# Sixteen heads of 8: rounds of two steps, the two second products behind each other, and one job of 128 rows per round

## The chip, the cores and the metric

The program runs on one core of one Trainium2 chip. The time is the device time of one execution in microseconds (us), the median of three runs. Five engines of the core take part, each with its own queue of instructions: TensorE (PE; PEld are its weight loads), ScalarE (ACT), VectorE (DVE), GpSimd (POOL) and SyncE (SP), which starts most DMAs.

## The reference

A stack of eight layers over `x` (16 batches, 256 tokens, 128 features), alternately attention with a context `ctx_512` (16 batches, 1601 keys, 64 features) and a feed-forward layer. The change touches three of the attention layers, those with 16 heads of 8:

```python
# first: causal self-attention and cross attention, added before the output projection
q, k, v = heads(x @ Wq + bq), heads(x @ Wk + bk), heads(x @ Wv + bv)
att = where(causal, einsum('bhqd,bhkd->bhqk', q, k) * scale, -inf)
y = einsum('bhqk,bhkd->bhqd', softmax(att), v)
qc, kc, vc = heads(x @ Wcq + bcq), heads(ctx @ Wck + bck), heads(ctx @ Wcv + bcv)
y = y + einsum('bhqk,bhkd->bhqd', softmax(einsum('bhqd,bhkd->bhqk', qc, kc) * scale), vc)
return y @ Wp + bp
# second and fourth: the cross part alone
```

Each is applied to the normalised `x` and added to it. The other layers (two experts' stages, a quantised convolution, an attention with heads of 32 and its own feed-forward parts, a shared expert) are not touched.

## The kernel before, in words

`attention8` writes one such layer; it is called three times, as stages a0 (with causal attention), a1 and a3 (cross attention alone). A quad is 4 heads; there are 4 quads for each source of keys. A step is one tile of 128 keys of one quad, against all 256 queries: 13 tiles for the context (the last has 65 keys) and 2 for the layer's own tokens. So a batch has 52 steps, or 60 in a0.

What a step does, with its letter in the plan:

- "scores" (L598 to 612): four matmuls of 64 contracted rows and 256 columns, on two halves of the array (`a` = 0, 1), transposed scores of 4 heads, into two of three score banks. They wait until ScalarE has done all halves up to the first one of the step before: `pe.wait_ge(S["probs"], 2 * e.i - 1)` (L602). With the split in three bf16 parts and a row for minus the maximum in the contraction, they come out shifted.
- The exponentials (L681 to 690): ScalarE takes each half, 128 x 512, from its bank into one of four buffers of probabilities.
- "pv" (L613 to 628), the second product, fp32: four matmuls, each on its own 32 columns of the array and all 128 rows, 9 outputs (8 and the sum) by 256 queries, added up in one bank over a quad. In the order before it comes `LAG8` = 3 steps after its scores. At a quad's end ScalarE copies the bank (L695).

Beside the steps runs the search for the maxima, a quad or so ahead. A "unit" (L575 to 597) is a matmul of 63 rows and 512 key columns into one of three banks, and VectorE reduces it to a column of maxima (L747). There are 26 per cross quad (24 full ones and two narrow ones, L738), two per step. After a quad's last unit VectorE forms minus the maxima (L751), TensorE transposes them (the job "turn", L635), ScalarE copies them (L701) and starts a DMA into the operand of the scores (L679).

All other matmuls are "jobs" that share one bank, `side_bank`: keys and values of the next batch from its context ("k_cross" L640, "v_cross" L644, with 64 rows, on one half of the array), and jobs of 128 rows: "turn", "x_turned" L649, "q" L652, "k_own" L654, "v_own" L657, "quad_out" (L662, transposes a quad's outputs), "heads_turned" L665, "proj" L668. Each waits until the one before it has been evacuated (L631, the semaphore `side_done`), by ScalarE (L696 to 726), or for "quad_out" and "proj" by VectorE (L769 to 792).

The order is a list of events that `schedule8` builds once; each engine walks the same list and takes what is its own. `segment8` writes one batch's part: for every step n its scores, two units, the second product of step n - 3, further units, then what was put at n. Jobs are placed by numbers of steps, so two or three can stand between two second products and the next scores, and keys and values come every second step. GpSimd splits keys and queries in bf16 parts (L512 to 518), SP writes and restacks them in DRAM.

## Time and profile before

| | us |
|---|---|
| runs | 7690.1, 7738.05, 7750.57 |
| median | 7738.05 |
| span of the profiled execution | 7680.6 |
| TensorE / VectorE / ScalarE / GpSimd busy | 6854.6 / 5897.9 / 4972.7 / 2316.8 |
| mean granted clock of TensorE | 0.951 |

The profile is of one execution of its own; of that one only the span, from its first to its last instruction, is given, and no time beside it. The runs are other executions. Busy times are sums over the span in which the union of an engine's instructions is counted; a matmul's end is modelled. Reductions of VectorE and exponentials of ScalarE overlap by some 0.05 to 0.1 us in the records, so starts are better than durations for a cadence.

### The profile page before, as it was taken

What the parts mean: (1) busy time and instruction counts of PE and PEld (TensorE: products, weight loads), DVE (VectorE), ACT (ScalarE), POOL (GpSimd) and SP (SyncE); (2) the same over time, 40 slices, a digit from 0 to 9 for tenths busy, and PEclk for the clock granted to TensorE, in tenths of its full rate; (3) what the DMA queues carried; (4) which work ended last, traced back from release to release, by engine and by line L of the source; (5) the groups of instructions that cost most, each with busy time, mean ns of one, the idle gap of its engine ahead of it and who ended that gap; (6) DMA issues with size and microseconds to landing.
All of it is one profiled execution on the core that took longest, in us unless ns stands there. A gap on an engine that the chain in (4) does not pass through costs nothing. (4 is left out here: it accounts for less than half of the span.)

```text
span 7680.6 us, 186325 instructions
## 1 busy us (share of the span) xinstructions
PE 6854.6 (89%) x73814; PEld 3108.2 (40%) x73814; DVE 5897.9 (77%) x12885; ACT 4972.7 (65%) x9846; POOL 2316.8 (30%) x2368
## 2 busy tenths in 40 slices
PE   6999999977999998788769999999996889999979
PEld 2333333343333333344424444444444433333335
DVE  6888888846898997788757777777774488999955
ACT  4787788834888886455446666666653168888842
POOL 1222222111211210155435555555554112212100
PEclk9999999987999999899879999999998589999989
DMA  5344444104434341100100000000001144343400
GB/s 101 86 98 94 94 91 94 44 27 84 95 78 103 81 92 44 28 18 17 40 22 10 9 8 10 6 10 9 5 5 56 28 103 99 75 103 85 85 26 12
DMA packets 319830, 417.82 MB, mean 54 GB/s; under 512 B 56533, under 2 KB 238054, under 8 KB 318969
## 3 DMA queue, kind: packets, MB, share of 16 engines
q1 hardware_dynamic: 317432, 405.36, 23.2%
q8 instruction: 595, 9.75, 0.6%
q14 instruction: 267, 2.18, 0.1%
q10 hardware_dynamic: 1536, 0.53, 0.0%
HBM read 225.41 MB, written 174.66 MB: 52 GB/s over the span
## 5 line engine op out<-in xcount | busy, mean ns | idle before, releaser
L688 ACT ACTIVATE a_probs<-scores_ps 128x512 f32<-128x512 f32 (+2 forms) x5248 | 2821.1, 591 | 356.9 <-PE scores_ps L608 263.7
L747 DVE TENSOR_REDUCE a_unit_max<-bank 128x1 f32<-128x512 f32 x3072 | 2003.7, 683 | 180.2 <-PE bank L595 145.3
L625 PE MATMUL bank<-a_probs,a_v_sb 128*9 128x256 f32 (+1 forms) x20992 | 1615.8, 380 | 29.3 <-ACT a_out_sb L695 20.3
L1299 ACT ACTIVATE cross_probs<-scores_ps 128x512 f32<-128x512 f32 (+1 forms) x1792 | 868.6, 571 | 590.4 <-PE scores_ps L1194 590.4
L608 PE MATMUL scores_ps<-a_stack 64*128 64x256 bf16 (+1 forms) x10496 | 1131.7, 275 | 60.9 <-ACT a_probs L688 55.9
L1381 DVE TENSOR_REDUCE cross_unit_max<-bank 128x1 f32<-128x512 f32 x1536 | 979.2, 685 | 253.3 <-PE bank L1180 250.2
L747 DVE TENSOR_REDUCE a_unit_max<-scores_ps 128x1 f32<-128x512 f32 x1536 | 1049.8, 683 | 160.4 <-PE scores_ps L595 143.1
L595 PE MATMUL bank<-a_stack 63*128 63x512 bf16 (+2 forms) x3413 | 1039.7, 372 | 7.4 <-DMA a_stack<-a_stack_dram 2.1
L1465 POOL TENSOR_TENSOR cross_added<-cross_probs 128x1024 f32<-128x1024 f32 x384 | 905.6, 2358 | 327.3 <-PE bank L1227 241.5
L608 PEld LDWEIGHTS scores_ps<-a_stack 64*128 64x128 bf16 (+1 forms) x10496 | 373.3, 96 | 991.1 <-ACT a_probs L688 831.7
L512 POOL CAST a_parts<-a_qk 128x512 bf16<-128x512 f32 (+3 forms) x225 | 117.7, 523 | 1893.8 <-ACT a_qk L707 1814.2
L595 PE MATMUL scores_ps<-a_stack 63*128 63x512 bf16 (+2 forms) x1707 | 635.7, 372 | 49.2 <-DMA a_stack<-a_stack_dram 45.9
L625 PEld LDWEIGHTS bank<-a_probs,a_v_sb 128*9 128x9 f32 (+1 forms) x20992 | 317.1, 88 | 700.2 <-ACT a_probs L688 397.1
L1191 PE MATMUL scores_ps<-cross_qk_f 32*128 32x256 f32 x6656 | 559.2, 394 | 8.6 <-ACT cross_probs L1299 8.5
L1218 PE MATMUL bank<-cross_probs,cross_v_sb 128*32 128x256 f32 x6656 | 452.3, 386 | 0.0
L1180 PE MATMUL bank<-cross_qk_b 32*128 32x512 bf16 x1536 | 390.4, 382 | 59.0 <-DVE cross_unit_max L1381 53.9
L805 POOL TENSOR_SCALAR_AFFINE_SELECT a_probs<-a_probs 128x512 f32<-128x512 f32 x128 | 81.3, 635 | 1014.1 <-ACT a_probs L688 1012.9
L595 PEld LDWEIGHTS bank<-a_stack 63*128 63x128 bf16 x3413 | 289.8, 94 | 185.6 <-DVE a_unit_max L747 59.5
L1191 PEld LDWEIGHTS scores_ps<-cross_qk_f 32*128 32x128 f32 x6656 | 312.5, 181 | 62.2 <-issue 28.7
L1194 PE MATMUL scores_ps<-cross_negmax_row,cross_ones_b 1*128 1x256 bf16 (+1 forms) x3328 | 297.2, 270 | 0.0
L1485 POOL CAST cross_qk_b<-cross_qk_f 128x1024 bf16<-128x1024 f32 (+1 forms) x128 | 109.1, 852 | 451.3 <-ACT cross_qk_f L1326 257.3
L640 PE MATMUL bank<-a_ctxT,a_wk_c_by_dim 64*128 64x512 f32 (+1 forms) x384 | 197.1, 595 | 52.6 <-DVE a_attn L779 24.4
(421 smaller groups left out, 10031.3 us busy)
## 6 DMA issues: line engine op xcount, KB each, us to landing
a_stack_dram<-a_parts SPq DMA_DIRECT2D x288, 400.2 KB, 4.3
a_stack<-a_stack_dram SPq DMA_DIRECT2D x256, 348.2 KB, 8.0
a_stack<-a_stack_dram SPq DMA_DIRECT2D x128, 444.2 KB, 9.9
a_ctxT<-in_ctxT SPq DMA_DIRECT2D x48, 400.2 KB, 4.8
a_stack_dram<-a_parts SPq DMA_DIRECT2D x288, 64.0 KB, 2.4
a_stack_dram<-a_parts SPq DMA_DIRECT2D x96, 128.0 KB, 2.4
f_x<-x_after_dram SPq DMA_DIRECT2D x32, 256.0 KB, 3.3
x_after_dram<-a_res SPq DMA_DIRECT2D x48, 128.0 KB, 4.3
```

The costliest lines, as they stand in the source:

```text
L595: ins = pe.matmul(bank[:, 0:n], stack[b][rows(a, 63), 2 * e.g + j, c0 + qt * P:c0 + (qt + 1) * P], stack[b][rows(a, 63), 2 * e.g + j, k0:k ...
L608: ins = pe.matmul(score_bank[(2 * e.i + a) % 3][0:n, j * TOK + q0:(j + 1) * TOK], stack[p][rows(a, 64), 2 * e.g + j, k0:k0 + n], stack[p][ ...
L625: ins = pe.matmul(out_bank[32 * h:32 * h + V8, q0:TOK], v[0:n, e.t, 4 * e.g + h, :], A.probs[0:n, held, o + q0:o + TOK], start=(e.t == 0), ...
L688: act.activation(by_pair(A.probs[0:n, b, a * 512:(a + 1) * 512])[:, :, q0:TOK], by_pair(score_bank[(2 * e.i + a) % 3][0:n, :])[:, :, q0:TO ...
L747: ins = dve.tensor_reduce(unit_max[:, e.g % 2, qt, 2 * a + j, c:c + 1], bank[:, 0:e.s.chunks[c][1]], AX.X, ALU.max)
L1180: ins = pe.matmul(bank[:, 0:n], q[rows(h), qt * P:(qt + 1) * P], k[rows(h), c0:c0 + n], start=True, stop=True)
L1191: pe.matmul(score_bank[h][0:n, m * TOK:(m + 1) * TOK], k[rows(h), k0:k0 + n], q[rows(h), :], start=True, stop=False, skip_group_check=True)
L1194: ins = pe.matmul(score_bank[h][0:n, m * TOK:(m + 1) * TOK], ones_b[D32 * h:D32 * h + 1, 0:n], row[D32 * h:D32 * h + 1, :], start=False, s ...
L1218: pe.matmul(out[:, 0:TOK], v[0:n, t, cols], probs[0:n, b, h, m, :], start=opens, stop=False, skip_group_check=True)
L1299: act.activation(probs[0:n, b, h, 0:m, :].rearrange("p m q -> p (m q)"), score_bank[h][0:n, 0:m * TOK], ACT.Exp, scale=scale).then_inc(S[" ...
L1381: ins = dve.tensor_reduce(unit_max[:, e.g % 2, qt, h, c:c + 1], bank[:, 0:n], AX.X, ALU.max)
L1465: pool.tensor_tensor(added[:, e.i % ADDS32, :, :], probs[:, b, :, 0, :], probs[:, b, :, 1, :], ALU.add).then_inc(S["added"], 1)
```

## The change

`plan8` takes the place of `segment8`. It lays out all batches in one list, in rounds of two steps, n0 even. A round holds, in this order: scores(n0), its units, then for the other engines the first half of the exponential, the "late" events and the second half, then "first" jobs (keys, values) with their evacuations; scores(n0+1), its units, its exponentials; then the second products of all steps below n0 (of the round before; at a quad's end also that of n0), then "rest" (splits, normalisation, DMAs) and at most one "last" job, of 128 rows. The evacuation of a last job is a late event of the next round. A last job that finds its round taken goes to the next. The units run six steps ahead instead of four, and minus the maxima have two buffers.

```diff
-LAG8 = 3
-SPACE8 = 4
+SPACE8 = 6
-        self.negmax = sb("negmax", [P, QT, 4])
+        self.negmax = sb("negmax", [P, 2, QT, 4])
...
+    def first(n, kind, b, **k):
+        e = put(n, "first", kind, b, **k)
+        evac(n, "first", e)
+
+    def last(n, kind, b, **k):
+        n += n % 2
+        while n in taken:
+            n += 2
+        taken[n] = kind
+        e = put(n, "last", kind, b, **k)
+        evac(n + 2, "late", e)
+        return n
...
+        for c in range(len(cross.chunks)):
+            first(ahead + 2 * c, "k_cross", b, c=c)
+            put(ahead + 2 * c, "rest", "split", b, j=c)
...
+        n = last(ahead + 4, "x_turned", b)
+        n = last(n + 2, "q", b)
...
+        for j in range((cross.T + 3) // 4):
+            first(ahead + 10 + 2 * j, "v_cross", b, j=j)
...
+    for n0 in range(-end, max(n for n, _ in at) + 2, 2):
+        core = 0 <= n0 < total
+        for half in range(2):
+            n = n0 + half
+            if core:
+                s, g, t = steps[n % end]
+                halves = [Ev("exp", s=s, g=g, t=t, i=n, part=a) for a in range(2)]
+                plan.append(Ev("scores", s=s, g=g, t=t, i=n))
...
+            plan += units_at.get(n, [])
+            if core:
+                plan.append(halves[0])
+            if half == 0:
+                plan += at.get((n0, "late"), [])
+            if core:
+                plan.append(halves[1])
+            if half == 0:
+                plan += at.get((n0, "first"), [])
+        if 0 <= n0 <= total:
+            upto = n0 + int(n0 < total and steps[n0 % end][2] == steps[n0 % end][0].T - 1)
+            for i in range(gone, upto):
+                s, g, t = steps[i % end]
+                plan.append(Ev("pv", s=s, g=g, t=t, i=i))
...
+        plan += at.get((n0, "rest"), []) + at.get((n0, "last"), [])
...
-                if e.kind in SIDE8 and e.kind not in ("quad_out", "proj"):
+                if e.kind == "evac" and e.job.kind not in ("quad_out", "proj"):
+                    e = e.job
...
-                if e.kind == "quad_out":
+                if e.kind == "evac" and e.job.kind == "quad_out":
+                    e = e.job
...
                     if e.last:
                         dve.wait_ge(S["max_taken"], e.u + 1)
+                        if e.read:
+                            dve.wait_ge(S["side_ps"], e.read)
```

The waits of the scores on the exponentials, the three score banks, the three banks of units, the side bank and the four buffers of probabilities are as before.

How the instructions stand now. First TensorE in stage a1, four plain steps before the end of a batch (L608 scores, L595 units, L625 second product; in the changed kernel L639, L626, L656). Before:

```order
L608 MATMUL scores_ps<-a1_stack1 128x256 x4
L595 MATMUL bank3<-a1_stack0 128x512
L595 MATMUL scores_ps<-a1_stack0 128x512
L625 MATMUL bank0<-a1_probs,a1_v_sb01 9x256 x4
L608 MATMUL scores_ps<-a1_stack1 65x256 x4
L595 MATMUL bank2<-a1_stack0 128x512
L595 MATMUL bank3<-a1_stack0 128x512
L625 MATMUL bank0<-a1_probs,a1_v_sb01 9x256 x4
```

and in the changed kernel, TensorE at such a place of stage a1:

```order
L639 MATMUL scores_ps<-a1_stack1 128x256 x4
L626 MATMUL bank2<-a1_stack0 128x512
L626 MATMUL bank3<-a1_stack0 128x512
L639 MATMUL scores_ps<-a1_stack1 128x256 x4
L626 MATMUL scores_ps<-a1_stack0 128x512
L626 MATMUL bank2<-a1_stack0 128x512
L656 MATMUL bank0<-a1_probs,a1_v_sb01 9x256 x8
L639 MATMUL scores_ps<-a1_stack1 65x256 x4
```

A second product stood between any two scores; now only two units stand between the first and the second scores of a round, and both second products before the next round's.

Second, TensorE in a1 where a batch's third lot of keys is made (L640, now L671) and a quad's outputs are transposed (L662, now L693). Before:

```order
L608 MATMUL scores_ps<-a1_stack0 128x256 x4
L595 MATMUL bank3<-a1_stack0 128x512
L595 MATMUL scores_ps<-a1_stack0 128x512
L625 MATMUL bank0<-a1_probs,a1_v_sb00 9x256 x4
L640 MATMUL bank1<-a1_ctxT1,a1_wk_c_by_dim 128x512
L608 MATMUL scores_ps<-a1_stack0 128x256 x4
L595 MATMUL bank2<-a1_stack0 128x512
L595 MATMUL bank3<-a1_stack0 128x512
L625 MATMUL bank0<-a1_probs,a1_v_sb00 9x256 x4
```

and after, TensorE in a1 at the same lot of keys:

```order
L656 MATMUL bank0<-a1_probs,a1_v_sb00 9x256 x8
L693 MATMUL bank1<-shared_ident,a1_out_sb 128x128 x2
L639 MATMUL scores_ps<-a1_stack0 128x256 x4
L626 MATMUL bank3<-a1_stack0 128x512
L626 MATMUL scores_ps<-a1_stack0 128x512
L671 MATMUL bank1<-a1_ctxT1,a1_wk_c_by_dim 128x512
L639 MATMUL scores_ps<-a1_stack0 128x256 x4
L626 MATMUL bank2<-a1_stack0 128x512
L626 MATMUL bank3<-a1_stack0 128x512
L656 MATMUL bank0<-a1_probs,a1_v_sb00 9x256 x8
```

The keys moved from behind the second product to between the first units and the second scores, and the job ahead of them on the side bank is now the outputs' transposes of the round just before.

Third, VectorE in a1 around that evacuation of a quad's outputs (the reciprocal and the product, L773 and L776 before, L807 and L810 now; reductions of units are L747 and L778). Before:

```order
L747 TENSOR_REDUCE a_unit_max<-bank 128x1 x2
L773 RECIPROCAL a_inv<-bank 128x8
L776 TENSOR_TENSOR a_attn<-bank,a_inv 128x4x2x8
L747 TENSOR_REDUCE a_unit_max<-scores_ps 128x1
L747 TENSOR_REDUCE a_unit_max<-bank 128x1
```

and in the changed kernel, VectorE in a1:

```order
L141 TENSOR_SCALAR a_xn<-a_x,a_ln_mv,a_ln_rs 128x128 x2
L778 TENSOR_REDUCE a_unit_max<-bank 128x1 x2
L807 RECIPROCAL a_inv<-bank 128x8
L810 TENSOR_TENSOR a_attn<-bank,a_inv 128x4x2x8
L778 TENSOR_REDUCE a_unit_max<-scores_ps 128x1
```

VectorE's own order is nearly the same. What moved is where it stands against TensorE's: the evacuation is behind the two units of the round's first step, and their matmuls stand between the transposes and the keys.

Counted over TensorE's rows of one batch in the middle: a batch of 52 steps has 26 rounds and 12 last jobs (4 "turn", 4 "quad_out", "x_turned", "q", "heads_turned", "proj"). Its keys and values are in 8 rounds, and the job in the round before them is: none, none, "quad_out", "x_turned" (keys, the fourth of 65 columns); "turn", "proj", "quad_out", "q" (values, the fourth of 65). Two "quad_out" stand directly behind the last second product of their quad. A batch of 60 steps has 30 rounds and 22 last jobs (8 "turn", 8 "quad_out", and one each of "x_turned", "q", "k_own", "v_own", "heads_turned", "proj"); before its keys stand four "quad_out" of causal attention, before its values "turn", "heads_turned", "proj" and "quad_out".

## Rows read from the trace of the kernel before

**Rows 1.** The page, busy us (share of the span) and instructions of each engine.
```profile
PE 6854.6 (89%) x73814; PEld 3108.2 (40%) x73814; DVE 5897.9 (77%) x12885; ACT 4972.7 (65%) x9846; POOL 2316.8 (30%) x2368
```

**Rows 2.** Windows: one batch of a1, two of a0, between writes of the result.
```profile
core 0: us, PE busy (x) PEld busy (x) DVE busy (x) ACT busy (x) POOL busy (x), PEclk, DMA share, GB/s
2240.03:2314.39 74.36, 71.70 (x816) 27.31 (x818) 67.42 (x125) 63.25 (x124) 14.34 (x22) 1.00 0.40 89
...
946.58:1129.88 183.30, 171.69 (x1936) 67.70 (x1928) 162.41 (x410) 146.99 (x301) 44.54 (x60) 1.00 0.39 89
```

**Rows 3.** Timeline of a1, a plain step (start us, us, instruction, idle before).
```profile
2203.81 0.39 PE L608 MATMUL scores_ps<-a_stack 64*128 64x256 bf16 x4
...
2204.45 0.62 PE L625 MATMUL bank<-a_probs,a_v_sb 128*9 128x256 f32 x8
2204.59 0.68 DVE L747 TENSOR_REDUCE a_unit_max<-scores_ps 128x1 f32<-128x512 f32 x1
...
2205.00 0.40 PE L608 MATMUL scores_ps<-a_stack 64*128 64x256 bf16 x4
...
2206.39 0.68 DVE L747 TENSOR_REDUCE a_unit_max<-scores_ps 128x1 f32<-128x512 f32 x1
```

**Rows 4.** Timeline of a1, a step whose engines waited for its scores.
```profile
2328.09 0.39 PE L608 MATMUL scores_ps<-a_stack 64*128 64x256 bf16 x4
...
2328.32 0.38 PE L595 MATMUL scores_ps<-a_stack 63*128 63x512 bf16 x1
...
2328.57 4.56 ACT L688 ACTIVATE a_probs<-scores_ps 128x512 f32<-128x512 f32 x8 [0.91 <-PE scores_ps L608]
2328.63 0.62 PE L625 MATMUL bank<-a_probs,a_v_sb 128*9 128x256 f32 x8
2328.80 0.69 DVE L747 TENSOR_REDUCE a_unit_max<-scores_ps 128x1 f32<-128x512 f32 x1
```

**Rows 5.** Timeline of TensorE in a1's last steps, which have no units.
```profile
3014.20 0.39 PE L608 MATMUL scores_ps<-a_stack 64*128 64x256 bf16 x4 [0.20 <-ACT a_probs L688]
3014.52 0.62 PE L625 MATMUL bank<-a_probs,a_v_sb 128*9 128x256 f32 x8
3015.34 0.39 PE L608 MATMUL scores_ps<-a_stack 64*128 64x256 bf16 x4 [0.20 <-ACT a_probs L688]
```

**Rows 6.** Timeline of TensorE: a quad's transposes and the scores behind them.
```profile
2211.01 0.44 PE L662 MATMUL bank<-shared_ident,a_out_sb 128*128 128x128 f32 x2
...
2211.38 0.39 PE L608 MATMUL scores_ps<-a_stack 64*128 64x256 bf16 x4
```

**Rows 7.** Timeline: the projection, the scores behind it, its evacuation.
```profile
2313.11 0.71 PE L668 MATMUL bank<-a_w_plain,a_attnT 128*128 128x128 f32 x4
...
2313.76 0.39 PE L608 MATMUL scores_ps<-a_stack 64*128 64x256 bf16 x4
2313.87 0.48 DVE L787 TENSOR_TENSOR a_x_res<-a_x_res,a_b_out 128x128 f32<-128x128 f32 x2
...
2314.39 0.42 DVE L790 TENSOR_TENSOR a_res<-bank,a_x_res 128x256 f32<-128x256 f32 x1
```

**Rows 8.** Timeline: an evacuation by ScalarE and the job that waits for it.
```profile
1026.13 0.40 ACT L714 ACTIVATE a_xnT<-bank 128x256 f32<-128x256 f32 x1
1026.58 0.44 PE L662 MATMUL bank<-shared_ident,a_out_sb 128*128 128x128 f32 x2 [0.54 <-ACT a_xnT L714]
```

**Rows 9.** Timeline: keys of 512 columns and the next second product.
```profile
1014.72 0.69 PE L640 MATMUL bank<-a_ctxT,a_wk_c_by_dim 64*128 64x512 f32 x1
...
1016.21 0.62 PE L625 MATMUL bank<-a_probs,a_v_sb 128*9 128x256 f32 x8
```

**Rows 10.** Timeline of VectorE: evacuation of a quad's outputs.
```profile
1010.96 0.20 DVE L773 RECIPROCAL a_inv<-bank 128x8 f32<-128x8 f32 x1
1011.19 0.22 DVE L776 TENSOR_TENSOR a_attn<-bank,a_inv 128x64 f32<-128x64 f32 x1
```

**Rows 11.** The addition for causal quads (ns min/median/max), and keys that waited for it.
```profile
L779 DVE TENSOR_TENSOR a_attn<-a_attn,a_more x64: 224/382/746, 188.3 to 1559.8; 128x64 f32<-128x64 f32 x64
...
1019.34 0.69 PE L640 MATMUL bank<-a_ctxT,a_wk_c_by_dim 64*128 64x512 f32 x1 [1.27 <-DVE a_attn L779]
```

**Rows 12.** Windows: a stretch of the stage with heads of 32, causal.
```profile
3500.00:3600.00 100.00, 84.04 (x910) 45.64 (x910) 79.52 (x174) 51.92 (x98) 52.17 (x55) 0.91 0.06 17
```

208 lines of the change are left out of this document (101 added, 107 removed).

## The prediction

> **What bounds the kernel now.** I read the page first. TensorE is busy for 89% of the span [rows 1], but a matmul's end is modelled, and two engines that wait for each other can both look busy. So I looked for the stages that the change touches, the three with heads of 8: the first (16 batches of 60 steps, cross and causal attention) and two with cross attention alone (16 batches of 52 steps). A table by windows, cut between two writes of the result tile, gives their periods: 74.4 us for a batch of 52 steps, 183.3 us for two batches of 60, so 91.65 each [rows 2]. In the short batch VectorE is busy 67.4 us and ScalarE 63.3 (with overlaps of neighbours), TensorE 71.7. The clock is 1.00 there, the level of 2.4 GHz. In all 32 x 74.4 + 16 x 91.65 = 3847 us, half of the span, hang on this cadence.
>
> Then a timeline of a quiet stretch. A step there takes 1.19 us (2203.81 to 2205.00), and VectorE starts its third reduction after 1.80 us, so one in 0.60; two units per step are 1.20 [rows 3]. The plain step is bound by VectorE. The step's own matmuls fit closely: scores to units 0.23, scores to second product 0.54 [rows 4], second product to next scores 0.55 [rows 3], sum 1.09.
>
> The row that decides is in the stage's last steps, where no units are left. TensorE has only scores and second products, 0.32 + 0.55 = 0.87 us, yet each step still takes 1.14, with 0.20 idle behind ScalarE's exponential [rows 5]. That is the loop scores, first exponential, next scores: the scores of step n+1 wait for the first half of step n (L602, since three score banks serve four halves). Scores to exponential are 0.48 [rows 4]; the rest, about 0.66, is the exponential and the way back. So two scores never follow each other in less than 1.14 us, whatever stands between them. Before, a whole step's work stands between them (1.09) and hides it.
>
> **The change part by part.**
>
> Plain round. Two steps are now scores, units, scores, units, two second products. Count from the round's first scores. Second scores: not before 1.14, since the units end at about 0.46 (two lots of 0.23) and 0.68 us stand empty; in front of the next scores nothing else may pass. Second products start 0.54 later, at 1.68. How long is the first of two back to back? No row shows a pair. Its ends are 0.31 (half of the 0.62 that a group's records cover) and 0.55 (no turn-round saved) [rows 3]. Units of two 512 columns cost 0.23 after scores of as many columns, and 0.31 before a second product [rows 4], so the turn costs some 0.08 and the product alone 0.55 - 0.08 = 0.47. I take 0.47. The next round starts at 1.68 + 0.47 + 0.55 = 2.70 us. Before it was 2 x 1.19 = 2.38. With the other ends it is 2.54 or 2.78. VectorE's four units (2.40) and ScalarE's four exponentials (7 starts in 4.56 - 0.60 us, 0.57 each, so 2.3) [rows 4] both fit below it. The saving of a turn is real, but it lies in front of a gap that was filled before.
>
> The Trainium skill, page "TensorEngine Tiling (Array Packing)", section "Key Properties", says that a change of the tiling mode drains the TensorE. The 0.08 above agrees in sign. By that rule alone the change should gain, one turn pair per round. The Trainium skill's page "TensorE: Matmul & The Clock Gate", section "The mechanism" under part 3, says that matmuls keep program order, start and end, and only weight loads are pulled ahead; by it nothing behind the second scores can fill the gap, as the 0.20 idle of rows 5 agrees.
>
> Jobs of 128 rows, at a round's end. They have the same cost as before, but now nothing hides them, since TensorE is on the path: 0.37 for two transposes [rows 6], 0.65 for a projection [rows 7]. A short batch has 10 of the first sort and 2 of the second (projection, queries): 3.7 + 1.3 = 5.0. A long batch has 18 and 5: 6.7 + 3.2 = 9.9. Their evacuations sit between the next round's exponentials, where ScalarE has room (2.3 + 0.4 below 2.70).
>
> Quad outputs. Two per short batch stand directly behind the third second product of their round and wait for ScalarE's copy of those very columns: the product's records take 0.62, the hand-over of a ScalarE result is about 0.45 (copy 0.40 and 0.05) [rows 8]. That is 1.1 from the product's start instead of 0.5: 2 x 0.6 = 1.2. In long batches other jobs take these places; 0.
>
> Half-row jobs (keys and values of the next batch, 8 per batch), between the first units and the second scores, where the gap is. Keys take 1.49 us from their start to the second products, scores and units of the step included, against 0.54 without them [rows 9]; values I take alike. If the side bank is free they start at 0.46 and the products at 1.95 instead of 1.68: only 0.27 each. This is the gain of the change: before they cost 0.9 each. But there is one side bank, and every job waits until the one before is evacuated, which is now the job of 128 rows from the round before, evacuated inside this round. Three cases:
> - evacuated by ScalarE: behind the first exponential, 0.48 + 0.55 + 0.45 = 1.48; products at 2.97, +1.3.
> - a quad output, evacuated by VectorE behind the round's first two units: first reduction at 0.23 + 0.48 = 0.71 [rows 4], two of them until 1.91, then 0.23 + 0.22 [rows 10] and 0.05, so 2.4; products at 3.9, +2.2. With causal attention's quads one more addition, 0.38 in the middle, +2.6. Such a wait is in the trace already: keys 1.27 us behind that addition [rows 11].
> - the projection, on VectorE too: 1.91 + 0.52 + 0.42 + 0.05 = 2.9 [rows 7]; products at 4.4, +2.7.
> By the order of TensorE's rows a short batch has two free ones (0.5), one behind ScalarE (1.3), two behind quad outputs (4.4), one behind the projection (2.7), and two narrow ones (65 keys) behind ScalarE, which I put at half, 1.3: 10.2. A long batch has three behind the longer quad outputs (7.8), two behind ScalarE (2.6), one behind the projection (2.7), two narrow ones behind quad outputs (half of 2.6 and 2.2 at least, and they wait for VectorE all the same; 2.9): 16.0. At the least all find the bank free: 8 x 0.27 = 2.2.
>
> The rest I cost at nothing. The causal quads' rounds hold up to eight short units, which lengthen a round, and narrower tiles shorten it; both below 1 us each. Keys are split, written and stacked later within the batch, around step 16 instead of 12, and are needed at step 33; at 1.6 us per step that covers 27 us. If this cover is gone, the units of the next batch wait for the stack, some us per batch, and scores behind them. The residual load and the result's store keep their order on SP's queue; the maximum rows have six steps instead of four before the scores that need them. The second copy of the row maxima takes a wait off nobody that waits now.
>
> **The sum.** Short batch: 26 x 2.70 + 5.0 + 1.2 + 10.2 = 86.6, against 74.4: +12.2. Long batch: 30 x 2.70 + 9.9 + 16.0 = 106.9, against 91.65: +15.25. In all 32 x 12.2 + 16 x 15.25 = 390 + 244 = +634 us. The profiled execution has a span of 7680.6; the runs shown lie at 7690 to 7751, their median 57 above the span. I add the difference to the median: 7738 + 634 = 8372, so 8370 us.
>
> **The rivals.**
> - Waits for the side bank stay small (VectorE ready earlier, or its units late enough to let the evacuation through): short batch 70.2 + 5.0 + 1.2 + 2.2 = 78.6, long 81.0 + 9.9 + 2.2 = 93.1; +134 + 23, 7895 us. For it: in short batches TensorE hardly waits for VectorE's evacuations now, though they are queued among units too. Against: both engines run their queues in program order, and the units stand ahead of the evacuation. Chance 0.09.
> - Same time: the pair of products is at its short end (round 2.54) and the bank is free; short 74.4, long 88.3, 7738 - 54 = 7685; inside 1% of before. Chance 0.04.
> - Faster: TensorE's turns are the bound, not the loop. The place is the pair of second products; each round gives back one turn and what waits around it. 71.7 of 74.4 us busy in the short batch speak for it [rows 2]. If each round saved 2 x 0.08 plus the 0.10 that separates 1.19 from 1.09 per step, it would be 0.36 x 26 = 9.4 per short batch and 10.8 per long one; but VectorE's 67.4 busy holds the short batch at 68 or so, 6.4 saved: 7738 - 32 x 6.4 - 16 x 10.8 = 7360. It decides if scores can be issued less than 1.14 after the last. Rows 5 deny it. Chance 0.05.
> - Clock: TensorE stands idle for up to 2 us in the rounds that wait for the bank. A stage of this kernel with TensorE 84% busy has a granted clock of 0.91 [rows 12], so nearly a fifth of it at 1.2 GHz. If a fifth of the 4480 us that these stages would take ran at half speed, with TensorE's work on the path for 1.56 of 2.70, that costs half of 900 x 0.58, 260; a tenth costs 130; I take 190: 8560. (The Trainium skill's page "TensorE: Matmul & The Clock Gate", section "HAM oscillation", says that gaps between bursts of matmuls lead there.) Chance 0.12.
>
> My forecast has 0.70. A measurement of this kernel tells about 1%, 77 us, from no change. Faster by over 1%: 0.05; within 1%: 0.04; slower by over 1%: 0.91. For the range I take the round of 2.54 with half of the side bank's waits as the lower end (8370 - 0.16 x 1312 rounds = -210, and -100), 8060, and the clock's case as the upper, 8580.
>
> **What would show it.** The same table by windows between two writes of the result: 86 to 87 and about 107 us per batch. In a quiet stretch scores at 0 and 1.14, then 2.70. ScalarE idle some 0.4 us per round behind scores, VectorE 0.3 behind units. In the list of waits, keys and values behind VectorE's attention tile and result tile, some 1.5 to 2.5 us longest, 5 or 6 times a batch. Wrong it would be if two scores stood nearer than 1.1 us, if keys' jobs started right behind the units in nearly all rounds, or if batches took under 80 us.

## The result and the profile after

The changed kernel takes 9112.6 us, the median of four runs (9082.3 to 9135.2); the kernel before took 7714.1 us beside it (7685.3 to 7750.6). The ratio is 1.181, with an interval of 1.177 to 1.186: slower, as forecast, but by 1398 us where 634 were forecast, and far outside the range of 8060 to 8580.

The page of the changed kernel, TensorE's busy time against [rows 1], and the granted clock in 40 slices (lines of the page's parts 1 and 2):

```profile
PE 7281.1 (80%) x73814; PEld 3397.4 (37%) x73814; DVE 5930.8 (65%) x12885; ACT 4979.5 (55%) x9846; POOL 2322.1 (25%) x2368
...
PEclk9888888888788888898797999999996688888889
```

Two things stand in these two lines. The number of matmuls is that of before, but they are busy 426 us longer (7281.1 against 6854.6), and the clock below says why. And the share of TensorE fell from 89 to 80%, since the span grew by 1452.8 us: some 1030 us are time in which it does nothing.

The windows by batch, as in [rows 2]: three batches of 60 steps and two of 52, between writes of the result tile. Columns: window, us, then busy us and instructions of TensorE, weight loads, VectorE, ScalarE and GpSimd, the granted clock, DMA share, GB/s.

```profile
884.35:1012.21 127.86, 96.45 (x964) 40.33 (x964) 80.55 (x206) 73.53 (x150) 22.35 (x30) 0.84 0.30 64
1012.21:1143.49 131.28, 99.74 (x964) 40.29 (x964) 80.59 (x205) 73.70 (x150) 22.32 (x30) 0.79 0.30 63
1143.49:1273.32 129.83, 98.05 (x964) 40.80 (x964) 80.59 (x206) 73.62 (x150) 22.32 (x30) 0.83 0.29 64
2819.11:2921.90 102.79, 77.12 (x812) 32.43 (x812) 68.71 (x125) 63.26 (x123) 14.50 (x22) 0.88 0.29 65
2921.90:3024.29 102.39, 78.54 (x812) 33.13 (x812) 68.63 (x126) 63.22 (x123) 14.51 (x22) 0.87 0.28 65
```

A short batch takes 102.6 us (86.6 forecast, 74.4 before), a long one 129.7 (106.9 forecast, 91.65 before). VectorE and ScalarE do what they did. The clock is 0.79 to 0.88 where it was 1.00.

A plain round, from the timeline of the changed kernel (start, duration, instruction, idle time before it and its releaser):

```profile
2968.66 0.39 PE L639 MATMUL scores_ps<-a_stack 64*128 64x256 bf16 x4
...
2969.80 0.39 PE L639 MATMUL scores_ps<-a_stack 64*128 64x256 bf16 x4 [0.53 <-ACT a_probs L718]
...
2970.38 1.05 PE L656 MATMUL bank<-a_probs,a_v_sb 128*9 128x256 f32 x16
2971.36 0.38 PE L666 MATMUL bank<-shared_ident,a_negmax 128*4 128x128 f32 x2
```

Scores at 0 and 1.14, second products at 1.72, and what follows the round (here a job) at 2.70: the loop is as it was read from [rows 5], to the hundredth, and so is the round.

The longest waits of TensorE in the stages with heads of 8, over the whole execution (total us, times, longest; shorter groups and those of other stages left out):

```profile
PE scores_ps L639 <- ACT a_probs L718: 465.9, 962, 0.8
PE scores_ps L639 <- DMA a_stack<-a_negmax_row: 163.7, 43, 7.6
PE bank L671 <- DVE a_attn L813: 111.4, 56, 2.6
PE bank L671 <- DVE a_attn L810: 104.8, 28, 3.8
PE bank L675 <- DVE a_res L825: 94.0, 42, 2.2
PE bank L675 <- DVE a_attn L810: 78.7, 45, 1.8
...
PE bank L675 <- ACT a_negmax_row L732: 34.6, 45, 0.8
```

and the first two of these groups in the kernel before:

```profile
PE scores_ps L608 <- ACT a_probs L688: 55.9, 258, 0.4
...
PE scores_ps L608 <- DMA a_stack<-a_negmax_row: 3.1, 2, 2.4
```

The first row is the loop. The rows from the third on, keys (L671) and values (L675) behind the evacuation of the side bank, were forecast. The second was not: scores waiting for the DMA of the maximum row, 43 times, up to 7.6 us; the kernel before has two such waits, 3.1 us in all.

Where the clock went, one short batch cut at the places where its level changes (same columns):

```profile
2922.00:2942.00 20.00, 16.59 (x102) 7.64 (x104) 7.11 (x13) 7.43 (x15) 2.10 (x4) 0.51 0.39 145
2942.00:2956.00 14.00, 9.47 (x123) 3.79 (x120) 9.60 (x17) 8.93 (x17) 0.00 (x0) 0.97 0.87 148
2956.00:2960.00 4.00, 3.23 (x28) 1.14 (x28) 2.42 (x4) 2.17 (x4) 0.00 (x0) 0.57 0.68 133
2960.00:3006.00 46.00, 35.34 (x432) 14.37 (x424) 38.77 (x72) 33.86 (x65) 7.28 (x10) 1.00 0.14 24
3006.00:3011.00 5.00, 4.57 (x30) 1.58 (x31) 1.63 (x5) 1.66 (x3) 3.00 (x5) 0.66 0.00 0
3011.00:3024.00 13.00, 9.34 (x114) 4.61 (x109) 8.74 (x17) 9.17 (x19) 2.13 (x5) 1.00 0.01 1
```

The clock is at its lower level, 1.2 GHz, for some 27 of 102 us: 20 in the rounds that make the values, and 3 to 4 each behind the wait for the maximum row and behind a wait of the keys. What stands at the head of each is plain in the timeline:

```profile
2922.38 1.64 PE L675 MATMUL bank<-a_wv_c,a_ctxT 64*128 64x128 f32 x6 [2.24 <-DVE a_res L825]
...
2956.47 0.61 PE L639 MATMUL scores_ps<-a_stack 64*128 64x256 bf16 x4 [2.73 <-DMA a_stack<-a_negmax_row]
...
3006.43 0.69 PE L671 MATMUL bank<-a_ctxT,a_wk_c_by_dim 64*128 64x512 f32 x1 [3.75 <-DVE a_attn L810]
```

Scores take 0.61 in the second row where they took 0.39. In the last three of the four rounds with values a wait stands at the head of each (2.24, 1.75, 0.68 us) and the clock stays down through all three. The stretches differ from batch to batch: in the batch before this one the same three waits brought 10 us at the lower level, and a wait of 4.62 us for the row another 10:

```profile
2850.00:2861.00 11.00, 8.33 (x60) 2.62 (x62) 5.16 (x8) 4.72 (x9) 0.00 (x0) 0.53 0.79 142
```

In the 46 us of plain rounds it is 1.00, though each holds an idle 0.53: that gap alone does not lower it here.

### The profile page after: what moved, and what is told of

Read it like the earlier page. It is cut to its first block and busy times, and to the rows that moved or that the text cites. A ratio compares the mean times of both kernels' runs of the same rounds, so it can differ in the third digit from the quotient of the medians.

```text
span 9133.4 us, 186575 instructions
## 1 busy us (share of the span) xinstructions
PE 7281.1 (80%) x73814; PEld 3397.4 (37%) x73814; DVE 5930.8 (65%) x12885; ACT 4979.5 (55%) x9846; POOL 2322.1 (25%) x2368
## 5 line engine op out<-in xcount | busy, mean ns | idle before, releaser
L778 DVE TENSOR_REDUCE a_unit_max<-bank 128x1 f32<-128x512 f32 x3072 | 2019.1, 684 | 967.6 <-PE bank L626 955.6
L639 PE MATMUL scores_ps<-a_stack 64*128 64x256 bf16 (+1 forms) x10496 | 1281.3, 298 | 630.1 <-ACT a_probs L718 465.9
L656 PE MATMUL bank<-a_probs,a_v_sb 128*9 128x256 f32 (+1 forms) x20992 | 1580.2, 425 | 0.0
L778 DVE TENSOR_REDUCE a_unit_max<-scores_ps 128x1 f32<-128x512 f32 x1536 | 1051.4, 684 | 537.2 <-PE scores_ps L626 534.6
L626 PE MATMUL bank<-a_stack 63*128 63x512 bf16 (+2 forms) x3413 | 1143.2, 412 | 42.3 <-DVE a_unit_max L775 26.9
L639 PEld LDWEIGHTS scores_ps<-a_stack 64*128 64x128 bf16 (+1 forms) x10496 | 409.2, 100 | 1569.3 <-ACT a_probs L718 1121.7
L626 PE MATMUL scores_ps<-a_stack 63*128 63x512 bf16 (+2 forms) x1707 | 704.6, 413 | 66.9 <-DMA a_stack<-a_stack_dram 45.2
L656 PEld LDWEIGHTS bank<-a_probs,a_v_sb 128*9 128x9 f32 (+1 forms) x20992 | 471.4, 95 | 730.8 <-issue 326.1
L675 PE MATMUL bank<-a_wv_c,a_ctxT 64*128 64x128 f32 (+1 forms) x1248 | 259.6, 362 | 246.2 <-DVE a_res L825 94.0
L671 PE MATMUL bank<-a_ctxT,a_wk_c_by_dim 64*128 64x512 f32 (+1 forms) x384 | 231.9, 691 | 270.5 <-DVE a_attn L813 111.4
L626 PEld LDWEIGHTS bank<-a_stack 63*128 63x128 bf16 x3413 | 307.1, 102 | 191.3 <-DVE a_unit_max L778 68.1
L675 PEld LDWEIGHTS bank<-a_wv_c,a_ctxT 64*128 64x128 f32 (+1 forms) x1248 | 208.1, 248 | 338.7 <-DVE a_res L825 110.4
```

Source lines behind the costliest of these rows:

```text
L626: ins = pe.matmul(bank[:, 0:n], stack[b][rows(a, 63), 2 * e.g + j, c0 + qt * P:c0 + (qt + 1) * P], stack[b][rows(a, 63), 2 * e.g + j, k0:k ...
L639: ins = pe.matmul(score_bank[(2 * e.i + a) % 3][0:n, j * TOK + q0:(j + 1) * TOK], stack[b][rows(a, 64), 2 * e.g + j, k0:k0 + n], stack[b][ ...
L656: ins = pe.matmul(out_bank[32 * h:32 * h + V8, q0:TOK], v[0:n, e.t, 4 * e.g + h, :], A.probs[0:n, held, o + q0:o + TOK], start=(e.t == 0), ...
L675: ins = pe.matmul(side_bank[0:n, t % 4 * P:(t % 4 + 1) * P], ctxT[b][:, k0:k0 + n], wv[0][:, :], start=True, stop=True)
L778: ins = dve.tensor_reduce(unit_max[:, e.g % 2, qt, 2 * a + j, c:c + 1], bank[:, 0:e.s.chunks[c][1]], AX.X, ALU.max)
```

## The experiments

Single runs; the kernel before ran beside them at 7685.9 to 7694.4 us, and the four runs of the changed kernel lie 53 us apart, so a difference below that says nothing. The edits are shown shortened. "Cold" below is the time in one short batch during which the granted clock was at its lower level, from windows of 2 us each. In the changed kernel it is 27, in the batch before that one 24.

**x1: the products apart again.** Each of a round's second products stands behind the units of one step; all else as changed.

```diff
-        if 0 <= n0 <= total:
-            upto = n0 + int(... last tile of a quad ...)
+            if 0 <= n0 <= total:
+                upto = n0 - 1 + half * (1 + int(... last tile of a quad ...))
```

> The changed kernel with one thing undone: a single second product behind the units of each step, instead of two behind each other; jobs, evacuations and their places stay. If the loop scores, exponential, next scores (1.14 us) is what makes the round long, plain rounds fall from 2.60 to about 2.4 us and the gap that lets the clock fall is gone: granted clock above 0.92, time 7900 to 8250 (what stays are the waits for the side bank, some 10 us per batch of 48). If the waits for the side bank and the clock they bring are nearly all of the loss, the time stays above 8500.

Measured 8920.6 us, 192 less; short batch 98.7, cold 27. The loop's waits go from 9.4 to 2.8 us in a batch, the waits for the side bank stay, and so does the cold time. The time stays above 8500, as the second expectation had it: the pairing is a small part.

**x2: the pairs alone.** The kernel before, its second products in pairs behind every second step, jobs where they were.

```diff
-        i = n - LAG8
-        if with_core and LAG8 <= n < end or with_tail and n < LAG8:
-            plan.append(Ev("pv", ...))
+        if n % 2 and n <= (end if with_core else 1):
+            ... both second products of the round before
```

> The kernel before with one part of the change alone: second products in pairs behind two steps of scores and units; jobs and evacuations stay where they were. Loop theory: plain rounds go from 2.38 to 2.60 us, 0.22 x 1312 = +290 us, about 8000, and more if the clock falls in the gaps, up to 8600. If turns of the array are what costs and the loss comes from the jobs' new places alone, the time is at or below 7714.

Measured 7942.0 us, 254 more than before; short batch 78.5, clock 0.98. Its plain rounds take 2.69 to 2.70 us, 0.32 more than two steps before. Over 1312 rounds that would be 420 us; jobs, which stand where they did, fill part of the gaps here (a round with a "turn" behind its first units, 2808.50 to 2811.20, takes 2.70 as well), so 254 is the price of the pairs alone.

**x3: plain gaps filled.** Six matmuls of no use in each round behind the first units.

```diff
+                if e.kind == "fill":
+                    for _ in range(6):
+                        pe.matmul(free score bank, 256 columns, ...)
```

> The changed kernel with six matmuls of 256 columns of no use added behind the first units of each round (0.64 us of work on one half of the array in the gap of 0.68), into a score bank that the second scores overwrite; they wait for the exponentials of the step before. Clock theory: about 700 of the 1400 us lost are the fall of TensorE's clock to 1.2 GHz for a quarter of the time, and busy gaps hold it: granted clock above 0.94, time 8350 to 8600. If the clock is only an effect and not a cause, or if half the array does not count, clock stays near 0.87 and the time at 9100 or above it.

Measured 9081.2 us, 31 less, which is within the spread; short batch 102.5, clock 0.88 as before, cold 24. A miss that tells something: the gap of the plain round is not what lowers the clock in the main. It may add to it: the granted clock of the whole execution is 0.895 where the four runs of the changed kernel have 0.871 to 0.879. But the filler also shortens the long waits (2.24 to 1.58 us, 3.75 to 2.62), so this run does not tell the two apart.

**x4: VectorE's evacuations first.** The evacuation of a quad's outputs or of the projection goes ahead of the round's first units on VectorE.

```diff
+            if half == 0:
+                plan += [e for e in late if by_dve(e)]
             ... scores, units, first exponential
-                plan += at.get((n0, "late"), [])
+                plan += [e for e in late if not by_dve(e)]
```

> The changed kernel with VectorE's evacuations of the side bank (quad outputs, projection) ahead of the round's first units in its queue instead of behind them. Side bank theory: TensorE's waits ahead of keys and values fall from 516 us (270 + 246) to under 200, and the clock recovers in part: 8500 to 8800. If these waits are hidden or come from elsewhere (GpSimd, normalisation), the time stays above 9000.

Measured 8588.0 us, 524 less; short batch 90.3, cold 7. The largest single repair. Its rows of waits:

```profile
PE bank L678 <- DVE a_attn L817: 71.5, 28, 2.6
PE bank L678 <- DVE a_attn L820: 62.7, 56, 2.5
...
PE bank L682 <- DVE a_attn L817: 4.1, 14, 0.3
```

The four rows behind VectorE were 388.9 us together (111.4 + 104.8 + 94.0 + 78.7) and are 138.3: 251 us less waiting, and 524 less time. Part of the 251 comes back elsewhere: the waits for the row rise from 163.7 to 212.6 us and those of the loop from 465.9 to 497.0. By the pages of the two profiles TensorE is idle 164 us less in all, and busy 383 less (6897.8 against 7281.1) with the same 73,814 matmuls in the same order. So more than two thirds of the gain is the clock. Its cold stretch stands at the wait for the row (3.93 us). A wait of 2.55 us for keys, at 2820.07, has none:

```profile
2820.00:2826.00 6.00, 5.05 (x62) 2.40 (x62) 4.32 (x10) 4.23 (x9) 5.05 (x8) 1.00 0.01 3
```

**x9: the waits filled.** No wait is taken away; TensorE runs matmuls of no use in them.

```diff
+    count = 4 in a plain gap; before keys or values: 20 or 30 (job before
+            evacuated by VectorE), 8 (by ScalarE); 22 before the third quad's scores
```

> The changed kernel with matmuls of no use (256 columns, half the array, some 0.11 us each) where TensorE stands idle: 4 in each round's gap, 20 to 30 more in the rounds whose keys or values wait for an evacuation by VectorE, 8 where they wait for ScalarE, and 22 before the one scores of a batch that waited 2.7 us for the maximum row. Nothing on the path is taken away. If the missing third of the loss is the clock, which falls to 1.2 GHz after such waits: the granted clock returns to 0.97 or more in the stages with heads of 8, a short batch takes 85 to 89 us in place of 102.6, and the whole 8400 to 8600 us. If the waits cost their own length and the clock is no more than a sign of them: 9050 to 9200 us, short batch 102 or more.

Measured 8860.1 us, 252 less, though TensorE does 222 matmuls more in a short batch (1034 against 812). Its windows: the rounds with values, the wait for the row, and a whole batch.

```profile
2665.00:2678.00 13.00, 12.41 (x138) 8.11 (x136) 6.31 (x12) 7.32 (x15) 1.70 (x4) 1.00 0.56 209
...
2694.00:2698.00 4.00, 4.00 (x34) 1.79 (x36) 2.58 (x4) 2.17 (x4) 0.00 (x0) 0.57 0.84 161
...
2664.31:2761.38 97.07, 91.47 (x1034) 49.97 (x1033) 68.71 (x125) 63.38 (x123) 14.48 (x22) 0.98 0.30 69
```

The rounds with values run at 1.00 and take 13 us where they took 20 at 0.51. Cold time is 3.5 us, behind the one wait that the filler did not cover (1.95 us left, for the row). This shows the clock as a cause and not a sign. It also shows that matmuls on half the array count for it, which x3 had left open. 8400 to 8600 us and 85 to 89 per short batch were expected; I had not counted that the filler takes the gap in which keys and values stood almost free (8 x 0.43 = 3.4 us a batch), which is only a part of what is missing.

**x7: single products and VectorE's evacuations first** (x1 and x4 together).

> The changed kernel with products single (as in x1) and VectorE's evacuations ahead of a round's first units (as in x4). If the loop (worth 192 us in x1, 254 in x2) and the side bank's waits with the clock behind them (524 us in x4) are separate and add up: 9112 - 192 - 524, some 8400 us. If the clock needs few or no long waits to hold, the two together give more: 8150 to 8300. If both are the same loss seen twice: about 8550.

Measured 8415.2 us, against 9112 - 192 - 524 = 8396: the two parts add up. Short batch 85.8, cold 3, at the wait for the row (4.16 us); a wait of 2.26 us for keys has no cold stretch.

**x8: keys and values behind the second products.**

```diff
-            if half == 0:
-                plan += at.get((n0, "first"), [])
...
+        plan += at.get((n0, "first"), [])      # behind the second products
```

> The changed kernel with keys and values behind the round's second products, where the evacuation they need is done, in place of the gap. By the theory of the side bank the waits of 2 to 4 us are gone; each of the eight jobs costs its 0.9 us on TensorE again, and some 1 us where a last job of the same round waits for its evacuation: warm 26 x 2.60 + 6.2 + 7.2 + 3 = 84 us in a short batch, and if the clock holds 8050 to 8300 us. If the clock falls also without these waits (through the gap of 0.53 in every round), 8500 us or more.

Measured 9025.3 us, 87 less. The time lies where the second expectation had it (8500 or more), but not for its reason, the gap alone. Short batch 102.6, cold some 24. The long waits for VectorE's evacuations are gone, that for the row (4.2 us) is not, and the last job of a round now waits 0.7 to 0.8 us for ScalarE's evacuation of the keys or values just ahead of it, behind the loop's 0.53 and beside units that wait up to 1.3 us. With waits of 0.83, 0.78, 1.32 and 0.78 us in one such run of rounds the clock is down for 14 us, so several middling waits in a row lower it as well as a long one does.

**x6: four score banks**, two for units.

```diff
+        score_bank = [S4[:, 0, 0], S4[:, 0, 1], S4[:, 1, 0], S4[:, 1, 1]]
+        max_bank = [G.bank[2], G.bank[3]]
-                        pe.wait_ge(S["probs"], 2 * e.i - 1)
+                        pe.wait_ge(S["probs"], 2 * e.i - 2)
```

> The changed kernel with four banks for scores and two for units: a round's second scores need not wait for the first exponential. By the loop theory plain rounds go from 2.60 to about 2.40 us (VectorE's four reductions), 5.2 us less in a short batch and 6 in a long one, 260 us: about 8850 us, with the side bank's waits and the cold stretches left. If units now wait for VectorE for want of a third bank, 9000 to 9200.

Measured 9400.7 us, 288 more, outside both expectations. In a short batch (116.2 us) the loop's waits are gone, and one of the same kind takes their place:

```profile
PE bank L626 <- DVE a_unit_max L778: 9.9, 27, 0.6
PE bank L671 <- DVE a_attn L810: 3.0, 1, 3.0
```

The waits for a third unit bank (9.9 us) are as long as those of the loop were (9.4). The loop theory is not tested by this run: units hold up what it freed. Nor do the waits explain its time. They are 23.8 us in this batch, as in the changed kernel's, but the clock is 0.79 where it was 0.87 (the next batch takes 110.2 us at 0.86), and over the execution TensorE is busy 7496.6 us, 215.5 more. Behind a wait of 1.57 us for the row it is at the lower level for 17 us:

```profile
2797.50:2814.70 17.20, 15.09 (x102) 4.74 (x102) 8.41 (x15) 7.08 (x15) 0.00 (x0) 0.50 0.55 92
```

Why the stretch is longer here is not shown.

**x10 and x14: the maximum row ahead of the restacking.** ScalarE starts the row's DMA at 2949.27; TensorE has it at 2956.47. SP began the eight restacking DMAs of the next batch 5 us before it:

```profile
2944.30 13.79 SPq L592 DMA_DIRECT2D a_stack<-a_stack_dram  x8
```

x10 moves the restacking's event six steps later in the plan:

```diff
-        put(n + 2, "rest", "stack", b)
+        put(n + 8, "rest", "stack", b)
```

> The changed kernel with the event that restacks the next batch's keys six steps later, so that the quad's maximum row is on its way before the restacking DMAs start. In the changed kernel TensorE waits 163.7 us in all, 43 times, for the row's DMA; issued at 2949.27 it was needed only at 2956.5, 7 us later, between restacking transfers. If that is the cause and each wait costs its own length: 9112 - 164, some 8950 us. If the clock falls behind each such wait too, as by the clock theory: 8700 to 8850. If the row is slow for another reason: no change, 9050 to 9150.

Measured 9107.2 us, no change, and the waits for the row are 171.2 us. By the code SP has nothing else in its queue to wait for there, so its DMAs start when their data is ready: the restacking follows the load of `x` directly (2531.66, 2533.01) as it did in the changed kernel (2942.34, 2944.30). The plan orders events, it does not time them. The theory was not tried. x14 holds them by the semaphore:

```diff
-                        if g == QUADS // 2 and e.after_row is not None:
+                        if g == 0 and e.after_row is not None:
                             sp.wait_ge(S[f"max_in{e.after_row % 2}"], rows_in(e.after_row))
```

> The changed kernel; the restacking DMAs of the next batch (eight transfers of 348 KB) now wait on a semaphore until the maximum row of the third quad has landed, where before only the last four of them did. If the row's DMA was late because it ran among these transfers: TensorE's waits for it (163.7 us) go, and the 3.5 to 4 us of cold clock behind each: 9112 - 164 - some 80, about 8870 us. If the restacking then comes too late for the next batch's units, 9000 us or more, with waits on the stack at units. If the row was slow by itself: 9100.

Measured 8953.5 us, 159 less. The row is issued at 2722.42 and the first restacking DMA, which waits until it has landed, at 2724.39: it takes under 2.0 us alone and 7.2 among the others. The wait is gone from the short batches; 84.9 us in 15 waits are left, most in the long ones. So 79 us of waiting less gave 159; 122 of it is busy time of TensorE (7158.7 against 7281.1). About 240 were expected. Half the waits stayed, and the clock did not recover everywhere: short batches take 101.8 and 96.1 us in turn, and in the first kind cold time is 34 us, more than before, with 14 at the wait of 3.74 us for keys:

```profile
2695.07:2796.89 101.82, 80.73 (x812) 33.81 (x812) 68.49 (x125) 63.25 (x123) 14.52 (x22) 0.83 0.29 65
2796.89:2892.97 96.08, 74.58 (x812) 32.05 (x812) 68.48 (x126) 63.20 (x123) 14.51 (x22) 0.91 0.31 69
```

In a long batch the late row is another one. In x14 the third quad's row is sent at 1036.70, the restacking follows at 1043.56, and a row sent at 1062.40 is waited for until 1069.49, with the DMA engines busy until shortly before:

```profile
1062.00:1066.00 4.00, 0.28 (x1) 0.09 (x1) 1.20 (x8) 0.96 (x3) 0.00 (x0) 0.72 1.02 156
```

That it is held up by the same restacking fits these times; no run holds the restacking behind that row.

**x11 and x15: all repairs.** x11 is x7 with x10's edit and the normalisation four steps earlier, so that it isn't ahead of the evacuation that the third keys need; x15 puts x14's semaphore in place of x10's edit.

```diff
-        put(ahead, "rest", "ln_stats", b)
...
-        put(ahead + 2, "rest", "ln_apply", b)
+        put(ahead - 4, "rest", "ln_stats", b)
+        put(ahead - 2, "rest", "ln_apply", b)
```

> x7 (single products, VectorE's evacuations first) with the restacking six steps later and the normalisation of the next batch four steps earlier, so that it does not stand before the evacuation that the third keys wait for. In x7 the row's DMA still cost 241.7 us of waiting and keys behind the attention tile 138. If only these lengths are gained: 8415 - 242 - some 60 = 8110. If the clock comes back with them (0.915 in x7): 7900 to 8050. None of it would explain a time below the kernel before, since one projection, turn or transposition per round stays on TensorE's path as before.

> x11 with the restacking behind the row, as in x14, by the semaphore. x11 still waited 237.7 us for the row: 8272 - 238 - some 80 = about 7950 us, granted clock 0.94. If the waits reappear at the units for want of the stack: 8150 or more. A time below the kernel before is not expected, since projection, turn and transpositions stay on TensorE's path without cover.

Measured 8272.3 us (x11) and 8131.0 us (x15), both above what was expected (8110 or less, and 7950). The normalisation was a cause: against x7 the waits of keys behind VectorE fall from 63.5 to 8.1 us (quad outputs) and from 74.5 to 49.4 (causal ones), and the time by 143. The row was still waited for 237.7 us in x11, since x10's edit has no effect. A short batch of x15, and of x11:

```profile
2621.16:2700.05 78.89, 70.96 (x812) 26.95 (x812) 66.83 (x126) 63.53 (x124) 14.42 (x22) 1.00 0.38 84
```
```profile
2384.72:2470.88 86.16, 72.59 (x812) 27.06 (x812) 66.92 (x125) 63.84 (x124) 14.38 (x22) 0.96 0.35 77
```

With the wait for the row, the last of over 2 us, the cold time of this batch goes too, and it falls from 86.2 to 78.9. What it still lacks against 74.4 is what stands open on TensorE: waits of 0.5 to 1 us behind ScalarE, and the jobs of 128 rows. Not every batch of x15 is as good, and the first stage is far from repaired:

```profile
893.35:1008.31 114.96, 99.53 (x968) 35.74 (x966) 80.91 (x206) 73.88 (x150) 22.43 (x30) 0.84 0.34 72
...
2778.84:2862.09 83.25, 74.52 (x812) 27.45 (x812) 66.95 (x126) 63.64 (x124) 14.40 (x22) 0.94 0.37 80
```

The five long batches from 893 to 1448 us take 108 to 115 us against 91.65 before. The first two have two waits for the row, 13.3 us together, and the clock at 0.84 and 0.88. This stage holds more than half of what x15 lacks. None of the fifteen kernels is faster than the one before.

**x12, x13 and x16: the price of one wait.** In the kernel before, TensorE is held once a batch at the third quad's first scores, until GpSimd has filled a tile three times; in x13 with 28 matmuls of no use in the hold; in x16 as x12, but on x2.

```diff
+                    if held_up(e):      # cross attention, third quad, first tile
+                        ... x13 alone: 28 matmuls of 256 columns
+                        pe.wait_ge(S["stall"], 3 * (e.i // steps_in) + 3)
```

> The kernel before with one wait of some 3 us put in per batch: at the first scores of the cross attention's third quad TensorE waits until GpSimd has filled a tile three times, begun when the scores could have started. Nothing else is moved. If a wait costs its own length: 48 x 3 to 4 us, 145 to 190 more than before, 7830 to 7880 us. If the clock falls to 1.2 GHz behind it for 15 to 20 us, as in the changed kernel, each costs 5 to 9 us more: 8050 to 8300 us, and the granted clock of these stages at 0.85 to 0.92.

> As x12, but 28 matmuls of no use (256 columns, half the array, some 3 us together) run on TensorE inside the same wait. The hold is the same, only TensorE is not idle. By the clock theory the clock stays where it is and only the length of the hold is lost: 7830 to 7900 us, granted clock 0.95 as before. If the loss of x12 comes from the other engines, which the hold starves alike, x13 takes as long as x12.

Measured 7927.9 us (+234) and 7846.1 us (+152). The scores behind the hold in x12, its windows at the hold and behind it, and a batch of x13:

```profile
2344.62 0.40 PE L618 MATMUL scores_ps<-a_stack 64*128 64x256 bf16 x4 [2.97 <-issue]
```
```profile
2341.00:2345.00 4.00, 1.03 (x16) 0.37 (x14) 1.44 (x3) 0.97 (x2) 2.86 (x3) 1.00 0.99 178
2345.00:2350.00 5.00, 4.97 (x45) 1.23 (x42) 3.75 (x6) 3.71 (x8) 0.00 (x0) 0.66 1.04 154
2350.00:2365.00 15.00, 14.97 (x183) 5.37 (x186) 14.75 (x29) 13.55 (x26) 0.00 (x0) 1.00 0.04 7
```
```profile
2300.26:2377.65 77.39, 74.65 (x844) 29.86 (x847) 67.55 (x126) 63.26 (x124) 17.20 (x25) 1.00 0.37 87
```

The wait of 2.97 us is followed by 3.5 us at the lower clock; filled, by none. The idle hold costs 234 / 48 = 4.9 us, the filled one 3.2: 1.7 us are the clock. Over the whole second stage the granted clock is 0.98 in x12 and 1.00 in x13. x13 came out as expected. x12 lies between its two expectations (7830 to 7880, and 8050 to 8300 by the clock theory), because I had carried 15 to 20 us of cold time over from the changed kernel; one wait among dense steps brings 3.5.

> x2 (the kernel before with its second products in pairs, 7942 us, with idle gaps of some 0.4 us in many rounds) with x12's wait of 3 us per batch. In the kernel before the wait cost 233 us, 81 of them not with TensorE kept busy (x13). If the time at the low clock depends on the wait alone: 7942 + 233, some 8175 us. If gaps in the plain rounds keep the clock low for longer, 10 us and more per wait: 8250 to 8400.

Measured 8070.6 us, 129 more than x2: neither expectation. The wait itself is 2.6 us, and the cold stretch behind it lasts 7 us where x12's lasted 3.5, which speaks for the gaps; but x2 has a cold stretch of 3.5 us of its own elsewhere in the batch that is looked at, and that one is missing here. How far gaps prolong a cold stretch stays open.

## Why the prediction was wrong

By the terms of its own sum, for a short batch, us:

| term | forecast | measured |
|---|---|---|
| 26 plain rounds | 70.2 | 70.0 (2.70; 2.60 to 2.66 with narrow units) |
| jobs of 128 rows | 5.0 | not measured again, 5.0 |
| quad outputs behind ScalarE's copy | 1.2 | 1.2 (two waits of 0.59) |
| keys and values, waits included | 10.2 | 12.3 (10.1 waited, 2.2 as at a free bank) |
| wait for the maximum row | 0 | 3.7 |
| sum at full clock | 86.6 | 92.2 |
| clock | 0 | not measured by itself; the rest to 102.6: 10.4 |

For a long batch the same gives 81.0 + 9.9 + 15.7 + 6.1, and 2.6 for units behind VectorE, 115.3; the rest to 129.7 is 14.4. Over 32 and 16 batches that is 948 us at full clock and 563 for the clock, against a difference of the spans of 1453 (the batches at the ends of a stage are shorter). Two other runs bear out the share of the clock. x2 has the same pairs at a clock of 0.936 and is busy 6727.3 us; the changed kernel is busy 554 us more with as many matmuls. And x9's short batch should take 92.2, 3.4 for the filler and 1.7 for one cold stretch as in x12, an estimate of 97.3; it takes 97.07.

- **The loop: right.** 1.14 between scores as in [rows 5], 0.53 idle. The round is 2.70 as forecast, made of 1.14, 0.58 (forecast 0.54) and a pair of products of 0.98 (1.02).
- **The side bank: right, with one thing left out.** The waits were forecast at 8.0 and 13.8 us beyond a free bank and measured 10.1 and 13.5; over all, 477 us were forecast (32 x 8.0 + 16 x 13.8) and the rows of waits for keys and values, the smaller ones with them, are 495. The left-out one is the normalisation in VectorE's queue. The third keys wait 3.75 us, not 2.2, since 1.96 us of it stand ahead of the units and the evacuation, and itself wait for GpSimd:

```profile
3002.85 1.96 DVE L141 TENSOR_SCALAR a_xn<-a_x,a_ln_mv,a_ln_rs 128x128 f32<-128x128 f32 x2 [0.71 <-POOL a_ln_rs L149]
3004.73 1.27 DVE L778 TENSOR_REDUCE a_unit_max<-bank 128x1 f32<-128x512 f32 x2
3005.93 0.19 DVE L807 RECIPROCAL a_inv<-bank 128x8 f32<-128x8 f32 x1
```

  The row "L141" stands at the head of VectorE's rows that the section on the change shows; I costed it at nothing. With the normalisation earlier (x11) nearly all of this wait is gone.
- **"The rest I cost at nothing": wrong in one item more.** "The maximum rows have six steps instead of four before the scores that need them." The steps were counted, not what else the DMAs do in them. Since the keys are restacked later, the restacking now runs when the third quad's row is sent; 164 us of waiting in all, 3.7 per short and 6.1 per long batch. x14 shows the cause for the short batches; for the long ones, where another row is late, it stays open.
- **The clock: the step that failed.** It stood among the rivals with 190 us and a chance of 0.12, and nothing in the likeliest case. Its size came from [rows 12], a stage with 84% of busy time and clock 0.91, by a share of a fifth to a tenth. But a mean share was the wrong measure. The clock follows where the waits are and how they lie: in the batch shown nothing behind the 0.53 of every plain round, 3 to 4 us at the lower level behind each lone wait, and 20 us through three rounds with a wait in each. Behind a lone wait of 2 to 5 us in the changed kernel's variants it was anything from nothing (2.55 us in x4, 2.26 in x7) to 14 us (3.74 in x14); only in x12, among dense steps, was it some 3.5 in nearly every batch. What decides the length within a batch stays open (x6, x14, x16). My own forecast had five or six such waits per batch, four of them in successive rounds; they should have been priced each with its cold time. The runs give that price: 251 us of waits less at the side bank gave 524 (x4), 79 at the row gave 159 (x14), a hold that costs 3.2 us filled cost 4.9 idle (x12, x13). By these runs each microsecond of long waits costs one and a half to two; set against all of TensorE's idle time, 164 us less in x4, it is three.

The Trainium skill's page "TensorE: Matmul & The Clock Gate", section "HAM oscillation", names waits between bursts of matmuls as what lowers the clock; x9 and x13 agree, since the same holds filled leave it at 1.00. Its section "A second HAM failure mode: psum-queue depth-cycling" has micro-idles between groups of matmuls do the same. For the plain rounds the trace does not show it: 46 us of them, an idle 0.53 in each 2.70, run at 1.00, and filling them (x3) gained 31 us of 9112. For somewhat larger idles it does: in x8 waits of 0.8 to 1.3 us in rounds in a row go with 14 us at the lower level.

## What to carry to other kernels

Price a wait of the matmul engine of over 2 us at one and a half to two times its length, or more where idle gaps lie around it, and waits in successive rounds as one cold stretch that lasts as long as they do; look at where they lie, not at the mean busy share. These are the figures of this kernel, and single stretches scatter widely around them. When an evacuation is moved into a queue behind work that needs the same engine's results, count everything ahead of it in that queue, normalisations and their producers included. And a step that moves DMAs to another time must be held against every small, urgent DMA that is issued there; an event's place in a plan holds nothing back unless something waits.

## What the runs showed that was not expected

- A quad's maximum row of 2 KB lands in under 2.0 us alone and in 7.2 among eight restacking DMAs of 348 KB, though it is issued from another engine's queue.
- In x12 a wait of 2.97 us is answered by 3.5 us at 1.2 GHz, and the fall comes when TensorE's work is already back (the window up to 2345 has 1.00, the scores come at 2344.62). It is not always so: in a long batch of x14 the clock falls within the wait itself, from 1062.34 to 1069.49 (0.72 in the window from 1062 to 1066).
- Useless matmuls in waits paid: x9 is 252 us faster than the changed kernel with 94 of them before the keys and values of each short batch.
- The kernel with all repairs takes 78.9 us in its best short batches at clock 1.00. The rival of small waits had 78.6, but for rounds with pairs of products; x15 has them single, so the agreement is luck.
